# Three attentions of a transformer kernel: part of the vector engine's row-maximum work and its normalisation go to GpSimd, and residual additions are made by pairs of tiles

## The reference

```
x = x + out_projection( softmax(q k^T * scale) v )     q from layer_norm(x), k and v from the context
A1: q and k are rotated by position (rope)      A2: one k and v head for all 16 heads, and biases
```

## Time and profile before

| | us |
|---|---|
| runs | 1471.62 (median), 1470.96 and 1475.32 |
| span of the profiled execution | 1467.0 |
| PE busy in it | 1171.7 (80%) |
| DVE busy | 988.9 (67%) |
| ACT busy | 667.1 (45%) |
| POOL busy | 538.9 (37%) |

### The profile page before, as it was taken

The page is one execution under the profiler, slowest core; times in us unless marked ns, Lnnn a source line. Parts: engine busy times, 40 slices in busy tenths (PEclk is TensorE's granted clock), DMA queues, the critical chain, the costliest instruction groups (busy, mean ns, idle before and its releaser), DMA issues. The chain is left out here.

```text
span 1467.0 us, 34935 instructions
## 1 busy us (share of the span) xinstructions
PE 1171.7 (80%) x11141; PEld 918.1 (63%) x11154; DVE 988.9 (67%) x2920; ACT 667.1 (45%) x1423; POOL 538.9 (37%) x590
## 2 busy tenths in 40 slices
PE   2699994439999957779987879999799956499991
PEld 1477773338899925556673456677477755399991
DVE  3689996474443347998984679888477777766552
ACT  1367762105555503345564546766234343144440
POOL 2324201664235256534411232431121125752554
PEclk9999997559999967899998989999799988599996
DMA  6887743012223258435532177564200042133542
GB/s 179 206 215 191 188 124 129 29 33 87 77 92 109 75 133 209 122 101 144 150 84 51 44 176 167 150 163 106 86 1 0 0 152 74 53 120 106 149 140 73
DMA packets 138978, 164.58 MB, mean 112 GB/s; under 512 B 15308, under 2 KB 118754, under 8 KB 131728
## 3 DMA queue, kind: packets, MB, share of 16 engines
q1 hardware_dynamic: 130664, 146.62, 37.0%
q0 software_dynamic: 8192, 16.46, 4.1%
HBM read 111.98 MB, written 51.38 MB: 111 GB/s over the span
## 5 line engine op out<-in xcount | busy, mean ns | idle before, releaser
L586 DVE TENSOR_REDUCE A_neg_max<-A_s_bank 128x4 f32<-128x512 f32 x384 | 253.2, 688 | 46.3 <-PE A_s_bank L725 35.9
L448 ACT ACTIVATE A_probsT<-A_st_bank 128x512 f32<-128x512 f32 x384 | 222.4, 602 | 40.4 <-PE A_st_bank L738 39.2
L725 PE MATMUL A_s_bank<-A_k_stack,A_q_stack 72*128 72x128 bf16 x1536 | 157.5, 228 | 38.0 <-DVE A_neg_max L586 22.3
L738 PE MATMUL A_st_bank<-A_q_stack,A_k_stack 128*128 128x128 bf16 x1536 | 153.1, 224 | 7.1 <-DVE A_q_stack L602 6.2
L738 PEld LDWEIGHTS A_st_bank<-A_q_stack,A_k_stack 128*128 128x128 bf16 x1536 | 112.5, 103 | 52.2 <-issue 42.9
L725 PEld LDWEIGHTS A_s_bank<-A_k_stack,A_q_stack 72*128 72x128 bf16 x1536 | 106.3, 102 | 52.1 <-DVE A_neg_max L586 33.4
L752 PE MATMUL A_pv_bank<-A_probsT,A_v_pad 128*32 128x128 f32 x3072 | 127.4, 284 | 1.5 <-issue 1.5
L2041 ACT ACTIVATE E_h<-E_h_bank,w_L_b 128x256 f32<-128x256 f32 x184 | 76.8, 471 | 72.4 <-PE E_h_bank L2141 71.0
L2153 PE MATMUL E_y_bank<-E_w,E_h 128*128 x736 | 90.3, 276 | 2.2 <-ACT E_h L2041 0.9
L752 PEld LDWEIGHTS A_pv_bank<-A_probsT,A_v_pad 128*32 128x32 f32 x3072 | 74.1, 111 | 24.7 <-issue 3.4
L2141 PE MATMUL E_h_bank<-E_xT,E_w_u 128*128 128x256 f32 x368 | 88.8, 386 | 0.0
(11 more groups left out here) (371 smaller groups left out, 2641.4 us busy)
## 6 DMA issues: line engine op xcount, KB each, us to landing
A_q_stack<-q_scratch SPq DMA_DIRECT2D x48, 576.0 KB
A_k_stack<-k_scratch SPq DMA_DIRECT2D x32, 576.0 KB
q_scratch<-A_q_parts SPq DMA_DIRECT2D x48, 192.0 KB, 2.3
A_k_stack<-k_scratch SPq DMA_DIRECT2D x48, 192.0 KB
E_xe<-slots_in SPq DMA_DIRECT2D x53, 128.0 KB, 2.1
slots_out<-E_ye SPq DMA_DIRECT2D x53, 128.0 KB, 1.7
A_ctxT<-in_ctxT SPq DMA_DIRECT2D x24, 256.0 KB, 10.5
k_scratch<-A_k_parts SPq DMA_DIRECT2D x32, 192.0 KB
```

The costliest lines, as they stand in the source:

```text
L448: act.activation(probsT[n % 2][:, c * HQ:(c + 1) * HQ, :], st_bank[c % 2][:, :].rearrange("k (a q) -> k a q", a=HQ), ACT.Exp, scale=scale) ...
L586: dve.tensor_reduce(neg_max[:, c * HQ:(c + 1) * HQ], s_bank[c % 2][:, :].rearrange("q (a k) -> q a k", a=HQ), AX.X, ALU.max, negate=True). ...
L725: last = pe.matmul(s_bank[c % 2][:, a * S:(a + 1) * S], q_stack[slot][0:COMBO, h, at:at + S], k_stack[slot][0:COMBO, h, at:at + S], start= ...
L738: last = pe.matmul(dst, k_stack[slot][:, h, at:at + S], q_stack[slot][:, h, at:at + S], start=True, stop=spread)
```

## The change

Four things change in `multi_head_attention`, in all of A0, A1 and A2 but for the second.

- `split_max` for tiles 2 and later goes from DVE to POOL. There are now two tiles neg_max, so that DVE can write one while POOL reads the other.
- In A0 and A2 (`BY_DVE = NH // 2`), DVE's `spread_max` writes under heads 0 to 7, and POOL's new `spread_rest` under heads 8 to 15. PE waits for the latter before the third quarter of `scoresT`. In A1, DVE still writes all 16.
- The normalisation of groups 3 and later goes from DVE to POOL; that of group 2 is made by DVE ahead of the loop, now in A1 too. The statistics stand in n0 and n1 in all three; in A1 they stood in n0, a group later.
- Instead of one `add_x` of 128 columns in each entry, DVE makes one `add_pair` of 256 columns in every second one (n0 and n2). The transposed maxima get columns of their own in the PSUM bank.

POOL's program is now written out by tile: in each entry the rest of the spread, then the split of the maximum, then what there was (late rows; `split_rest` for K in n1, for Q in n2; the bias), then in n3 the inverse deviation and the normalisation.

```diff
-    BY_DVE = NH
+    BY_DVE = NH if rope else NH // 2
...
-    if rope:
-        NORM_AHEAD = 2
-        STATISTICS, NORMALISE = {0: range(GB)}, {2: range(GB)}
-    else:
-        NORM_AHEAD = 3
-        STATISTICS, NORMALISE = {0: range(0, 2), 2: range(2, GB)}, {6: range(0, 2), 7: range(2, GB)}
+    NORM_AHEAD = 3
+    STATISTICS = {0: range(0, 2), 2: range(2, GB)}
...
+            def normalise(g):
+                pool.wait_ge(rstd_done, g + 1)
+                pool.wait_ge(prep_ready, U * (g - 1) + X + 1)
+                for j in range(GB):
+                    last = pool.tensor_scalar(xn[:, j, :], core.x_tile(g * GB + j), mv[g % 2][:, j, 0:1],
+                                              rstd[:, j:j + 1], ALU.subtract, ALU.mult)
...
+            def split_max(b):
+                pool.wait_ge(max_done, 4 * (b + 1))
+                pool.wait_ge(mt_ready, b)
+                own.link(pool.tensor_copy(max_parts[:, hi:hi + NH], neg_max[b % 2][:, :]))
+                pool.tensor_tensor(max_parts[:, lo:lo + NH], neg_max[b % 2][:, :], max_parts[:, hi:hi + NH], ALU.subtract)\
+                    .then_inc(m_split, 1)
...
+            def spread_rest(b):
+                if BY_DVE < NH:
+                    slot, at = b // 2 % 4, b % 2 * S
+                    pool.wait_ge(mt_copied, b + 1)
+                    pool.tensor_copy(q_stack[slot][MAX_ROWS, BY_DVE:NH, at:at + S],
+                                     max_rows[b % 2][MAX_ROWS, None, :].to_broadcast([2 * NH, NH - BY_DVE, S]))\
+                        .then_inc(m_spread_rest, 1)
...
+            inverse_deviation(2)
+            spread_rest(0)
+            for b in range(NB):
+                g = b // GB
+                if has_scores(b + 1):
+                    spread_rest(b + 1)
+                if has_scores(b + 2):
+                    split_max(b + 2)
+                if late:
+                    late_rows(*{0: (7, 10), 1: (10, 11), 2: (11, 12), 3: (12, 13), 4: (13, 16)}.get(b, (0, 0)))
+                if b % GB == 1 and exists(g + 2):
+                    split_rest(pool, own, k_f, k_parts, kd, g + 2, KL, k_lead, k_split)
+                if b % GB == 2 and exists(g + 2):
+                    split_rest(pool, own, q_f, q_parts, D, g + 2, QL, q_lead, q_split)
+                    add_bias(g + 2)
+                if b % GB == 3 and exists(g + 3):
+                    inverse_deviation(g + 3)
+                    normalise(g + 3)
...
-                    add_x.it = it
-                    add_x(b, n)
-                    if has_scores(b + 2):
-                        split_max(b + 2)
+                    if n % 2 == 0:
+                        add_pair.it = it
+                        add_pair(b, n)
...
+                if c * HQ == BY_DVE:
+                    pe.wait_ge(m_spread_rest, b + 1)
```

More of the change, by code:

```diff
@@ L148, in multi_head_attention @@
         stats = sb("stats", [S, GB, 6], F32)
-        mv = sb("mv", [S, GB, 2], F32)
+        mv = [sb(f"mv{i}", [S, GB, 2], F32) for i in range(2)]
         rstd = sb("rstd", [S, GB], F32)
@@ L152, in multi_head_attention @@
         xnT = sb("xnT", [D, GT], F32)
-        neg_max = sb("neg_max", [S, NH], F32)
+        neg_max = [sb(f"neg_max{i}", [S, NH], F32) for i in range(2)]
         max_parts = sb("max_parts", [S, MAX_ROWS.stop], BF16)
@@ L398, in _ @@
             split_rest(pool, own, q_f, q_parts, D, 1, QL, q_lead, q_split)
-            if late:
-                for g in range(2):
-                    late_rows(7 + 5 * g, 8 + 5 * g)
-                    inverse_deviation(g + 2)
-                    late_rows(8 + 5 * g, 10 + 5 * g)
-                    split_rest(pool, own, k_f, k_parts, kd, g + 2, KL, k_lead, k_split)
-                    late_rows(10 + 5 * g, min(12 + 5 * g, 16))
-                    split_rest(pool, own, q_f, q_parts, D, g + 2, QL, q_lead, q_split)
@@ L407, in _ @@
             for g in range(2):
                 add_bias(g)
-            if not rope:
-                inverse_deviation(2)
-                for g in range(2, NG):
-                    split_rest(pool, own, k_f, k_parts, kd, g, KL, k_lead, k_split)
-                    if exists(g + 1):
-                        inverse_deviation(g + 1)
-                    split_rest(pool, own, q_f, q_parts, D, g, QL, q_lead, q_split)
-                    add_bias(g)
-            else:
-                first = own.n
-                steps = 1 + 2 * 3
-                with pool.Fori(first_round, last_round) as it:
-                    for gg in range(2):
-                        own.start(first + ((it - first_round) * 2 + gg) * steps)
-                        inverse_deviation(it * 2 + gg + 2)
-                        split_rest(pool, own, k_f, k_parts, kd, it * 2 + gg + 2, KL, k_lead, k_split)
-                        split_rest(pool, own, q_f, q_parts, D, it * 2 + gg + 2, QL, q_lead, q_split)
-                        assert own.n == steps
+            inverse_deviation(2)
@@ L533, in _, with statistics @@
             dve.sem_inc(x_added, START)
+            own.did(dve.memset(wo_bank[:, 0:2 * D], 0.0))
             dve.memset(pv_bank[:, :], 1.0).then_inc(pv_done, CREDIT)
             own.wait()
-            def statistics(at, tiles=range(GB)):
+            def statistics(at, q, tiles=range(GB)):
+                if tiles[0] == 0 and not (isinstance(at, int) and at < 2):
+                    dve.wait_ge(xn_done, at - 1)
                 for j in tiles:
@@ L543, in statistics, with normalise @@
                 for j in tiles:
-                    last = dve.bn_aggr(mv[:, j, :], stats[:, j, :])
+                    last = dve.bn_aggr(mv[q][:, j, :], stats[:, j, :])
                 if tiles[-1] == GB - 1:
                     last.then_inc(stats_done, 1)
-            def normalise(g, at, tiles=range(GB)):
-                if tiles[0] == 0:
-                    dve.wait_ge(rstd_done, g + 1)
-                    dve.wait_ge(stats_done, g + 1)
-                    if not (isinstance(g, int) and g == 0):
-                        dve.wait_ge(prep_ready, U * (g - 1) + X + 1)
-                for j in tiles:
-                    last = dve.tensor_scalar(xn[:, j, :], core.x_tile(at * GB + j), mv[:, j, 0:1],
+            def normalise(g):
+                dve.wait_ge(rstd_done, g + 1)
+                dve.wait_ge(stats_done, g + 1)
+                if g > 0:
+                    dve.wait_ge(prep_ready, U * (g - 1) + X + 1)
+                for j in range(GB):
+                    last = dve.tensor_scalar(xn[:, j, :], core.x_tile(g * GB + j), mv[g % 2][:, j, 0:1],
                                              rstd[:, j:j + 1], ALU.subtract, ALU.mult)
-                if tiles[-1] == GB - 1:
-                    last.then_inc(xn_done, 1)
+                last.then_inc(xn_done, 1)
             def rotate(g, use, dst, parts, split, written, copies, lead):
@@ L591, in split_max @@
                 dve.wait_ge(max_done, 4 * (b + 1))
-                if not (isinstance(b, int) and b == 0):
+                if b > 0:
                     dve.wait_ge(mt_ready, b)
-                own.link(dve.tensor_copy(max_parts[:, hi:hi + NH], neg_max[:, :]))
-                dve.tensor_tensor(max_parts[:, lo:lo + NH], neg_max[:, :], max_parts[:, hi:hi + NH], ALU.subtract)\
+                own.link(dve.tensor_copy(max_parts[:, hi:hi + NH], neg_max[b][:, :]))
+                dve.tensor_tensor(max_parts[:, lo:lo + NH], neg_max[b][:, :], max_parts[:, hi:hi + NH], ALU.subtract)\
                     .then_inc(m_split, 1)
@@ L672, in place @@
                         if at in STATISTICS and exists(ahead):
-                            statistics(ahead, STATISTICS[at])
-                        if at in NORMALISE and exists(ahead):
-                            normalise(ahead, ahead, NORMALISE[at])
+                            statistics(ahead, (n // GB + NORM_AHEAD) % 2, STATISTICS[at])
                         for use, g in uses_at(at, it * 2 + n // GB):
```

94 lines of the change are left out of this document (54 added, 40 removed).

## The result

The changed kernel takes 1498.03 us (median of 4 runs, 1491.42 to 1501.96) against 1472.14 of the kernel before beside it. The ratio is 1.0171, with a 95% interval of 1.0141 to 1.0201: it is slower by 1.7%, some 26 us. I had forecast 1476, with a range up to 1490. The profiled execution took 1497.82 and has a span of 1496.0, which is 29.0 more than before. A run takes about 1.8 us more than its span (1497.82 - 1496.0), and before the median run took 4.6 more than the profiled span; so that profiled execution was some 3 us quicker than the median (an estimate), and the 29.0 holds these 3 us, the 26 do not. Every ratio here is of runs in the same, usual state; one run alone was not, of 3966.88 us in a version further down, and its ratio is of the other three.

The account below looks back on a forecast made before the run. PE and DVE were taken as both near their limit. A0 +2, A2 +4.5 and A1 -2 made +4.5 on a span of 1467.0, so 1471.5, and with 4.6 for the median run 1476 us; range 1458 to 1490.

Parts of the forecast that it names:

- What bounds the kernel: All three attentions: PE and DVE near their limit at once, so relief of one buys only what the other leaves.
- The floors of 4.66 and 5.30: Late A0, without DVE's statistics or normalisation: a tile without work for later groups takes 4.66 us, one holding V 5.30.
- Q tiles: Tiles holding Q's product (n2), 5.68 us in A0: held to be PE's own, no gain seen.
- The split on POOL: Split of the maximum on idle POOL: wake-up 0.17, two instructions of 0.27, gap 0.17; sum 0.9 us, bounds 0.8 to 1.6.
- the rival of a slow spread: POOL's spread at 1.5 us instead of 1.0 delays the maxima: +18, 1490; decides from about 1.25; chance 0.21.
- Bare tiles: Tiles without work for later groups (n3): split late behind POOL's Q split; 5.4 us in A0, 6.1 in A2.
- A1's groups: Four groups of A1 after its first round: 24.9 to 26.1 us each, +1.2 a group, +4.8 in four.
- The two lateness terms: A1's groups: POOL's split of the maximum comes 0.9 us late in n2 and 2.0 late in n3.
- the relief in n1: A1's groups: DVE relieved by 1.1 us a group, as normalisation stands between two products sharing one PSUM bank.
- The V tile: Tile holding V (n0): four POOL normalisations take 1.5 us, split about 0.2 late; 5.5 us, against 5.76 in A0, 5.91 in A2.
- A1's first round: Start of A1, taken as DVE's: -5 us for work leaving DVE and -1.8 for a load wait.
- The shared port: DVE's spread waits out POOL's two-input instruction: 1.0 us each, 6 for twelve n3 tiles, about half held in the terms.

Follow-up runs that it names:

- The runs in halves: Changed kernel, but POOL normalises two tiles of a group in n3 and two in n0 behind the split of the maximum: 1481.68 us, ratio 1.0063.
- with wide instructions: Changed kernel, but POOL normalises with two instructions of 128x512 instead of four of 128x128: 1483.64 us, ratio 1.0061.

## Why the prediction was wrong

**What bounds the kernel** was read rightly: PE and DVE are both near their limit, and relief is worth what PE leaves. The floors of 4.66 and 5.30 came true in A0 once the split stood on DVE ahead of the addition, and Q tiles did not move.

**The split on POOL** is two instructions of 0.20 and 0.22 us with a gap of 0.18, 0.60 without the wake-up that my 0.9 held. The spread took 1.034 where I had put 1.0, so the rival of a slow spread had its condition wrong, though its 1490 was nearest to the result.

**Bare tiles**: forecast 5.4 in A0 and 6.1 in A2, measured 5.18 and 6.16. The mechanism that I gave for the loss, the split behind POOL's splits of Q, is what the trace shows, though not alone: in two of the five tiles of A0 the last maximum was there 3.44 us into the tile and POOL's queue held the split until 5.22, in the other three DVE's spread had taken over 1.1 us beside POOL, and the maximum itself came at 4.1 to 4.4.

**A1's groups**: forecast 26.1, measured 26.40, and this nearness is in part luck. The two lateness terms came true, 0.98 us a group in n2 where I had 0.9 and 1.30 in n3 where I had 2.0 - 0.6. But the relief in n1 was 1.56 instead of 1.1, and the V tiles, for which the sum had no term, cost 0.81 a group; why is said below, under the clock.

**The V tile is the step that failed.** I took four normalisations on POOL at 1.5 us in all, between 0.23 and 0.61 each, and had n0's split come "about 0.2 late". They take 3.2 to 3.4 in A0 and A2. The reader can see the price on the tile's own row (ns minimum, median, maximum), POOL's 788 beside DVE's 343:

```profile
L371 POOL TENSOR_SCALAR A_xn<-x_sb,A_mv,A_rstd x60: 782/788/1282, 82.0 to 1005.1; 128x128 f32<-128x128 f32 x60
L583 DVE TENSOR_SCALAR A_xn<-x_sb,A_mv,A_rstd x36: 333/343/1067, 21.9 to 873.2; 128x128 f32<-128x128 f32 x36
```

The bounds were at fault, not only the value: they came from a 128x4 row and a cast of the earlier trace rows, neither of which has two operands per partition. DVE itself takes 0.343 for the form in the earlier trace rows, and no row says that POOL is at most 1.8 times as slow (0.61 by 0.343), so the upper end had no ground. The V tiles then cost 14.3 us in A0 and A2, where the sum had -2.6. That is 17 of the 24.5 us by which the growth of the span (29.0) passed my 4.5; with it alone put right the same sum gives 1493. The runs in halves (16 us) and with wide instructions (14 us) give this back.

The Trainium skill, GPSIMD Engine Reference, section on engine selection, calls one-input work on that engine roughly line-rate. POOL's casts and its copy follow one rate here: medians of 0.197 us for 16 columns, 0.609 for 512 and 1.034 for 1024 make 0.83 ns for each further column. The normalisation doesn't fit it: one tensor input of 128 columns with two operands per partition takes 0.788, 2.3 times what DVE takes, where that rate gives an estimated 0.29, while a two-input instruction of four times the columns takes 1.06 or 1.09 in the mean. The measurement decides; whether the 0.5 more is paid by the instruction or by the column no run shows.

**A1's first round**: I took DVE's work there as the limit and subtracted 5 for what leaves it, and 1.8 for a load. The round fell by 0.7. DVE's longest piece was six additions of 5.88 us beside POOL's split (2.29 elsewhere), and those stayed; the split of the maximum moreover went behind POOL's DMA issues, where POOL had no gap of over 0.45 us between 599 and 641 us. That is 6 us of the miss, less 2.6 that came at A1's end.

**The shared port** was priced too low. DVE's half of the spread takes 0.42 us alone, and in the Q and the bare tiles it meets the last instruction of POOL's splits of K and Q:

```profile
168.97 1.16 POOL L311 TENSOR_TENSOR A_k_parts<-A_split_r,A_k_parts 128x512 bf16<-128x512 f32 x1 [0.18 <-POOL A_k_parts L309]
169.05 1.36 DVE L628 COPY A_q_stack<-A_max_rows 32x1024 bf16<-32x1024 bf16 x1
```

Of DVE's 64 half spreads in A0 and A2, 20 took over 0.8 us, ten in Q tiles and ten in bare ones, all beside that instruction; the mean of the 64 is 0.67. The whole spreads of before had 0.71, with 2 over 0.8. So halving the copy saved 0.04 us instead of the 0.27 that I took: the added work on POOL ate it. With the split on DVE and POOL less crowded the mean is 0.54. With the whole spread back on DVE and split and normalisation on POOL it is 0.86, which is why the bare tiles of A0 did not gain there: in all five the spread took 1.25 to 1.68, and the last maximum came that much later.

**The clock** was in no step. After one wait for POOL in A0 the granted clock fell. The windows (columns as above) hold the tile before the wait, the wait, and two halves of the K tile behind it:

```profile
132.50:134.10 1.60, 1.60 (x31) 1.30 (x31) 1.54 (x4) 0.97 (x3) 1.60 (x3) 1.00 0.79 210
134.10:136.50 2.40, 0.38 (x4) 0.14 (x2) 0.31 (x1) 0.67 (x2) 1.74 (x4) 1.00 0.85 213
136.50:140.00 3.50, 3.46 (x31) 2.03 (x31) 2.72 (x9) 1.73 (x4) 1.03 (x1) 0.63 1.05 247
140.00:143.60 3.60, 3.60 (x51) 3.08 (x48) 1.48 (x3) 2.65 (x7) 1.14 (x3) 0.88 0.75 199
```

PE had done 0.38 us of work in 2.40; then it ran at 0.63 of full speed, that is for most of the stretch at 1.2 instead of 2.4 GHz, and the K tile took 7.09 instead of 5.69. Two K tiles of A2 (7.19 and 7.15) go the same way: 4 us in all. So do two V tiles of A1 (7.53 and 7.51, where the other two took 6.03 and 6.30), in which PE is busy throughout:

```profile
700.88:708.41 7.53, 7.53 (x82) 6.20 (x83) 5.51 (x13) 3.30 (x8) 5.24 (x8) 0.79 0.82 214
728.22:735.73 7.51, 7.51 (x82) 6.20 (x83) 4.94 (x9) 3.29 (x8) 5.15 (x8) 0.79 0.81 211
```

That makes some 7 us of the 29. In the kernel before the granted clock stayed at 1.00 from the second group of A0 and of A2 to their last transposition, and through A1's four groups. A lower clock does not follow each such wait: behind the one of 1.82 us that ends at 185.59 the K tile took 5.69. That the wait is the cause was not tested by itself; from the second group on, K tiles of 7 us and more stand in A0 and A2 only in the two kernels whose V tiles there took over 7 us in the mean.

**The chances.** I gave slower 0.39 and faster 0.25, with a centre on the upper edge of "no change". The range would have had to reach 1498. It ended at the one unknown cost that I had a rival for; the other unknown cost, in the same queue and four times a group, had none.

## What to carry to other kernels

An engine's idle share doesn't tell whether it can serve a waiting engine: add up what stands ahead of the awaited instruction in its queue, in each entry, and move only work whose result has a whole tile of time. Leave a wide upper bound on a form that the trace doesn't show on that engine, above all when it runs four times in a row ahead of something awaited. A large piece may be kept on the helper by cutting it in two at the awaited instruction, which gave back 16 of 26 us here, at the price of one wait of 5.7 us in A1's first round.

## What the runs showed of the hardware

On POOL a 128x128 subtract and multiply with two operands per partition takes 0.79 us, four of them 3.2 to 3.6; the same work as two 128x512 instructions with spread operands takes 1.06 and 1.09. The copy of 32x1024 bf16 takes 1.034.

DVE's row maxima don't stretch beside POOL, even in this kernel, while copies and two-input additions do (0.42 to over 1.3, 0.35 to 1.3):

```profile
L612 DVE TENSOR_REDUCE A_neg_max<-A_s_bank x384: 673/692/694, 44.9 to 1054.2; 128x4 f32<-128x512 f32 x192
```

The Trainium skill, SBUF — State Buffer, section on who interferes with whom, says that DVE's tensor_reduce never contends on this chip and that a DVE instruction with two inputs in SBUF contends with a GpSimd instruction that reads SBUF. The trace agrees with both, by this row and by the 5.88 us of six additions beside POOL's split.
